# A graph layer's first stage: 16-bit one-hots of several steps, a re-timed order, one scatter per expert tile

## What is computed

```python
def gat_layer(x, W, a_src, a_dst, b, src, dst, n):
    h = x @ W
    e = leaky_relu((h @ a_src)[src] + (h @ a_dst)[dst], 0.2)
    w = exp(e - segment_max(e, dst, n)[dst])
    alpha = w / segment_sum(w, dst, n)[dst]
    return segment_sum(h[src] * alpha[:, None], dst, n) + b
def gnn(x): return gat_layer(relu(gat_layer(x, W1, ...)), W2, ...)   # self loops added
x = x + gnn(layernorm(x))
x = x + ffn(layernorm(x))      # attention of 12 heads, then top-2 of 8 experts per row, GELU
```

## Time and profile before

| | us |
|---|---|
| median of 3 runs | 1517.9 |
| profiled execution, its own time | 1517.2 |
| its span, first to last instruction | 1515.5 |
| busy: TensorE / VectorE / ScalarE / GpSimd | 1400.4 / 1146.0 / 959.7 / 502.2 |

### The profile page before, as it was taken

The page is one execution under the profiler, slowest core; times in us unless marked ns, Lnnn a source line. Parts: engine busy times, 40 slices in busy tenths (PEclk is TensorE's granted clock), DMA queues, the critical chain, the costliest instruction groups (busy, mean ns, idle before and its releaser), DMA issues.

```text
span 1515.5 us, 25550 instructions
## 1 busy us (share of the span) xinstructions
PE 1400.4 (92%) x8885; PEld 1327.4 (88%) x8885; DVE 1146.0 (76%) x1760; ACT 959.7 (63%) x1653; POOL 502.2 (33%) x366
## 2 busy tenths in 40 slices
PE   2999799999799999899999999999998997799996
PEld 1897577999799999799999999999998897699996
DVE  5788889735699863386877878778788887788885
ACT  7997787523368432275848758487587421699895
POOL 1000000000000001153635636356376410388887
PEclk9999799999999999999999999999999998799999
DMA  7001000122214540000000000000010596376642
GB/s 203 1 1 31 12 12 20 52 94 73 92 64 135 178 154 1 21 1 1 22 0 21 0 0 21 0 21 0 0 32 22 156 300 138 122 166 159 158 93 39
DMA packets 52528, 99.14 MB, mean 65 GB/s; under 512 B 11064, under 2 KB 27068, under 8 KB 52440
## 3 DMA queue, kind: packets, MB, share of 16 engines
q1 hardware_dynamic: 39985, 72.60, 15.4%
q0 software_dynamic: 11376, 22.29, 7.6%
q10 hardware_dynamic: 1079, 3.13, 0.7%
HBM read 67.15 MB, written 44.31 MB: 74 GB/s over the span
## 4 chain that ended last, share of the span: by engine, by line
PE 69%; DVE 6%; issue 3%; ACT 2%; POOL 2%; DMA 1%; ACTq 0%; POOLq 0%; SPq 0%; DVEq 0%
PE ps L376 14%; PE ps L377 14%; PE ps L378 14%; PE ps L870 5%; PE ps L915 4%; PE ps L917 3%; PE ps L894 3%; PE ps L916 3%; PE ps L896 3%; DVE mcol L1139 1%; POOL prlo L1102 1%; PE ps L616 1%; PE ps L1328 1%; DVE prlo L1102 1%; PE ps L1752 1%
## 5 line engine op out<-in xcount | busy, mean ns | idle before, releaser
L1102 POOL TENSOR_TENSOR prlo<-prob,prhi 125x500 fp32r<-125x500 f32 x180 | 260.0, 1452 | 248.4 <-ACT prob L1040 248.0
L1139 DVE TENSOR_REDUCE mcol<-ps 125x1 f32<-125x1250 f32 x120 | 174.9, 1458 | 70.1 <-PE ps L870 68.6
L1038 ACT ACTIVATE prhi<-ps 125x500 fp32r<-125x500 f32 x300 | 176.7, 589 | 70.8 <-PE ps L896 63.9
L915 PE MATMUL ps<-prhi,vhi 125*128 125x250 f32 x600 | 171.5, 286 | 10.0 <-POOL prlo L1102 6.4
L1607 POOL MEMSET q<- 128x2500 f32 x1 | 2.2, 2184 | 526.7 <-PE ps L378 526.7
L1040 ACT ACTIVATE prob<-ps 125x500 f32<-125x500 f32 x300 | 176.3, 588 | 0.7 <-DVE prlo L1102 0.6
L917 PE MATMUL ps<-prlo,vhi 125*128 125x250 f32 x600 | 167.6, 279 | 0.0
L916 PE MATMUL ps<-prhi,vlo 125*64 125x250 f32 x600 | 166.6, 278 | 0.0
L894 PE MATMUL ps<-qst,kst 128*125 128x250 f32 x600 | 155.3, 283 | 2.7 <-ACT val L569 1.1
L376 PE MATMUL ps<-hhi,pthi 125*125 125x384 f32 x400 | 153.2, 383 | 3.0 <-DVE ptlo L742 3.0
L1752 PE MATMUL ps<-ohs,ohd 128*125 128x417 bf16 x380 | 125.6, 383 | 32.3 <-DVE ohs L2194 29.5
(11 more groups left out here) (336 smaller groups left out, 3996.8 us busy)
## 6 DMA issues: line engine op xcount, KB each, us to landing
w1all<-in_L_ffn_W_dram SPq DMA_DIRECT2D x8, 1152.0 KB, 8.9
w2st<-in_L_ffn_W_dram SPq DMA_DIRECT2D x8, 1152.0 KB, 6.7
wqst<-in_L_ffn_Wqkv_dram SPq DMA_DIRECT2D x12, 384.0 KB, 4.1
hid_d<-tin SPq DMA_DIRECT2D x10, 375.0 KB
hin<-hid_d SPq DMA_DIRECT2D x10, 375.0 KB
vtin<-xn_d SPq DMA_DIRECT2D x10, 375.0 KB
out_dram<-accr POOLq DMA_DIRECT2D x10, 375.0 KB, 8.5
xres<-in_x_dram SPq DMA_DIRECT2D x10, 336.0 KB
```

The costliest lines, as they stand in the source:

```text
L915: pe.matmul(ps[:, b:b + GQ], vhi[:, e, kt, :], hi, start=kt == 0, stop=False)
L1038: act.activation(prhi[:, n % RING, :], bank(3 + n % 3, P, 2 * GQ), ACT.Exp, scale=float(HD) ** -0.5)
L1102: eng.tensor_tensor(prlo[:, n % RING, :], prob[:, n % 3, :], prhi[:, n % RING, :].bitcast(f32), ALU.subtract)\
L1139: dve.tensor_reduce(mcol[:, e, t:t + 1], ps[0:P, 0:N], AX.X, ALU.max, negate=True).then_inc(sem("max"), 1)
```

## The change

Seven things change together.

1. The source one-hots of four steps are built by one VectorE instruction on 16-bit numbers, those of the destinations of 14, 12 and 12 steps likewise; the steps lie in pairs, so that two neighbouring 2-byte elements belong to two steps and a step's operand is read with a pitch of 4 bytes. The digit value is no longer in the source one-hot: ScalarE multiplies it into each step's destination one-hot in place (`valued`). `ohs` has 3 buffers of four steps, `ohd` 4.
2. The preparation is rearranged: three fused compares with sums for the flag ahead of the digits, 16-bit copies of the column numbers, constants in another order; the edges' large loads wait for nothing and go ahead of the weights, which move from ScalarE's queue to SP's.
3. Row statistics from row tile 2 on are VectorE's (`bn_stats`, `bn_aggr`).
4. The linear starts at step 8 and takes 12 steps per row tile; turns start at step 151 and take 31 steps.
5. The first aggregated tile of layer 1 is formed in 1125 and 125 columns, and the exponential's table is loaded beforehand.
6. The second layer's weights are split from `weight2_at(k)` on, behind the last step.
7. One indirect DMA per expert tile adds all its rows; it waits for the one before.

```diff
-FIRST, PERIOD = 31, 13
-TURN0, TURN, EARLY, SLOTS = 208, 32, 12, 21
-AHEAD = 30
+FIRST, PERIOD, PARTS = 8, 12, 13
+TURN0, TURN, EARLY, SLOTS = FIRST + 143, 31, 12, 21
+AHEAD = 20
+COUNT_READY = 8
 def linear(t, r):
-    return FIRST + PERIOD * t + r
+    return FIRST + PERIOD * (PARTS * t + r) // PARTS
+def weight2_at(k):
+    return max(turn_at(7, 17) + 7 * k, STEPS + 1 + 7 * k)
...
-    ohs = put("ohs", [128, OHS, WIDE], bf16, at=WEND)
+    ohs = put("ohs", [128, SRCS, SRC_WIDE // 2, PACK, 2], bf16, at=WEND)
+    ohd = put("ohd", [128, DSTS, DST_WIDE // 2, P, 2], bf16, at=ohs_end)
+    iota2 = put("iota2", [128, PACK, 2], f16, at=put.end)
+    scol = put("scol", [128, NCOLS], f16, at=put.end)
...
 # SP
+            for a, e in ((0, src), (1, dst)):
+                sp.dma_start(eraw[:, a, 0:2, :], ...).then_inc(sem("edges_in"), 16)
             sp.wait_ge(sem("set_pool"), ERAW_CLEAR)
...
+            for m in range(2):
+                sp.dma_start(wall[:, 3 * m:3 * m + 3, :], ...)
...
 # GpSimd
-            def add_first(j):
+            def add(j):
                 pool.wait_ge(sem("y_row2"), j + 1)
+                if j >= 1:
+                    pool.wait_ge(sem(f"added{(j - 1) % 3}"), 16 * ((j - 1) // 3 + 1))
                 pool.indirect_dma_start(out=out[:, :], ..., compute_op=ALU.add,
                                         bounds_check=N - 1, oob_is_err=False)\
-                    .then_inc(sem(f"add_first{j % 3}"), 16)
-            def add_second(j):
...
 # TensorE
                 if i == 0:
-                    pe.wait_ge(sem("ohd_ready"), b + 1)
-                pe.wait_ge(sem("oh_ready"), g + 1)
-                pe.matmul(into, hots(b)[:, i, :], ohs[:, g % OHS, 0:PACK], ...)
+                    pe.wait_ge(sem("oh_ready"), b + 1)
+                pe.wait_ge(sem("valued"), g + 1)
+                pe.matmul(into, hot_dst(g), hot_src(g), ...)
...
 # ScalarE
-                last = act.activation(hots(b)[:, i, :], iota[:, 0:P], ACT.Identity, bias=drel[:, j, u:u + 1])
+                act.activation(hot_dst(g), hot_dst(g), ACT.Copy, scale=sval[:, q:q + 1]).then_inc(sem("valued"), 1)
...
+                if g == NINE + 6:
+                    sloped(act, 0, 0, 0, NINTH)
+                if g == LAST_ES + 3:
+                    sloped(act, 0, 0, NINTH, N)
+                if g == EXP_LOAD:
+                    act.activation(stat[:, 0, 0:1], viol[0:P, 3:4], ACT.Exp)
...
 # VectorE
+            def destinations(b):
+                if b >= DSTS:
+                    dve.wait_ge(sem("oh_free"), dst_start(b - DSTS + 1))
+                dve.tensor_tensor(ohd[:, b % DSTS, 0:pairs, :, :],
+                                  iota2[:, 0:P, :].rearrange("p (o c) z -> p o c z", o=1).broadcast_to([128, pairs, P, 2]),
+                                  drel[:, j, DST_AT[i]:DST_AT[i + 1]].rearrange("p (b o z) -> p b o z", o=1, z=2)
+                                  .broadcast_to([128, pairs, P, 2]), ALU.is_equal).then_inc(sem("ohd_ready"), 1)
+            def moments1(t):
+                for h in range(2):
+                    order.did(dve.bn_stats(bn[:, t % 2, 6 * h:6 * h + 6], xall[:, t, h * HALF:(h + 1) * HALF]))
+                dve.bn_aggr(lnc[:, t, 0:2], bn[:, t % 2, :]).then_inc(sem("ln"), 1)
...
             def step_near(g):
-                dve.tensor_scalar(ohs[:, g % OHS, :], iota[:, 0:WIDE], scol[:, q:q + 1], sval[:, q:q + 1], ALU.is_equal, ALU.mult)
+                if i:
+                    return
+                if b >= SRCS:
+                    dve.wait_ge(sem("oh_free"), src_end(b - SRCS))
+                dve.tensor_tensor(ohs[:, b % SRCS, 0:wide // 2, :, :],
+                                  iota2[:, :, :].rearrange("p (o c) z -> p o c z", o=1).broadcast_to([128, wide // 2, PACK, 2]),
+                                  (scodd[:, q - ODD:q - ODD + wide] if STARTS[j] % 2 else scol[:, q:q + wide])
+                                  .rearrange("p (b o z) -> p b o z", o=1, z=2)
+                                  .broadcast_to([128, wide // 2, PACK, 2]), ALU.is_equal).then_inc(sem("oh_ready"), 1)
```

More of the change, by code:

```diff
@@ L149, in build @@
     mcol = put("mcol", [P, 2, T], f32)
-    viol = put("viol", [128, 4], f32)
+    viol = put("viol", [128, 6], f32)
     FREE = top[0]
@@ L210, in build @@
     lohi = put("lohi", [128, 3, ECOLS], f32, at=put.end)
+    digit = put("digit", [128, 3, NCOLS], f32, at=put.end)
     xres = put("xres", [P, 2, D], f32, at=W2AT)
@@ L296, in build @@
     etile = put("etile", [S, TILES], i32, at=put.end)
-    index = put("index", [S, 3, TILES], i32, at=put.end)
-    later = put("later", [S, 3, TILES], f32, at=put.end)
+    index = put("index", [S, 2, TILES], i32, at=put.end)
+    later = put("later", [S, 2, TILES], f32, at=put.end)
     twice = put("twice", [P, T], f32, at=put.end)
@@ new lines, in _ @@
+            for t in range(FIRSTS):
+                moments1(t)
+            act.wait_ge(sem("start_dve"), VALUES)
+            for g in range(4):
+                valued(g)
+            weights1(0)
+            for g in range(4, 8):
+                valued(g)
+            normed(0)
+            weights1(1)
+            for g in range(8, 12):
+                valued(g)
+            weights1(2)
+            higher1(0)
+            for k in range(3, KD):
+                weights1(k)
+                valued(9 + k)
@@ L1899, in _ @@
+            for g in range(15, AHEAD):
+                valued(g)
             for g in range(SCHEDULE):
@@ new lines, in _ @@
+            s_, d_ = edge[:, 0, 0:NCOLS], edge[:, 1, :]
+            third, node, value = (digit[:, i, :] for i in range(3))
+            real = slice(LEAD, LEAD + EROWS)
+            order.did(dve.scalar_tensor_tensor(lohi[:, 0, real], d_[:, real], 0.0, lohi[:, 0, real], ALU.add, ALU.is_lt,
+                                               accum_out=viol[:, 0:1]))
+            order.did(dve.scalar_tensor_tensor(lohi[:, 1, real], d_[:, real], 0.0, lohi[:, 1, real], ALU.add, ALU.is_ge,
+                                               accum_out=viol[:, 4:5]))
@@ L2166, in rest1 @@
                     .then_inc(sem("tile_yfree"), 1)
-            def destinations(b):
-                dve.wait_ge(sem("apart"), b + 1)
-                dve.tensor_scalar(hots(b), hots(b), 0.0, None, ALU.is_equal).then_inc(sem("ohd_ready"), 1)
             def finish1(t, u):
```

376 lines of the change are left out of this document (203 added, 173 removed).

## The result

The changed kernel takes 1509.4 us (median of five runs, 1508.0 to 1511.3) where the kernel before took 1517.9: a ratio of 0.9948, interval 0.9935 to 0.9960. It is faster by 8.5 us; the forecast was 19 us (1498). The time lies inside the wide range of 1477 to 1514, and just outside the 1487 to 1508 that the prediction gave its own mechanism. The profiled execution takes 1508.7 us with a span of 1506.9. Three slow executions of two later runs (1554.9, 1756.1 and 1992.8 us) are left out of every median here.

The account below looks back on a forecast made before the run. TensorE was taken to bound the linear and the sums without steps, with a chain through three engines between. Layer 1 falls from 334.4 to 317.5 us (16.9) and scatters start 2.3 earlier: 19.2 less, 1498 us, range 1477 to 1514.

Parts of the forecast that it names:

- Start and A: Everything before the linear's first triple: first count step at 20.3 us (was 25.3), first triple at 30 (was 44.6).
- The one-hots: Count steps on VectorE: one 4-byte pair per tick, 11.7 us per 38 steps, 1.1 less than before.
- The rival of one element per 1.04 ns: Packing fails: 38 steps cost VectorE 22.4 us, total 1601 us; chance 11% for unpacked or hopping together.
- 1.73 ns per column: Hopping source in the one-hot compares: 38 steps some 7 us dearer, total about 1557; chance 11% for unpacked or hopping together.
- ScalarE: A subtraction per step traded for a scaling, 380 for 380 at 0.30 to 0.39 us: zero net.
- B: From the linear's first triple to its last, TensorE the bound: 94 us, was 95.8.
- D1: From the first triple of the sums to the last count step, TensorE becomes the bound: 136 us, was 103.0.
- TensorE's pitch: Count matmuls reading 2-byte operands at a 4-byte pitch: nothing added; a spacing above 0.18 us would show a cost.
- C: From the linear's last triple to the first triple of the sums: 27 us (22 to 32), was 37.8.
- the rival of two tied engines: VectorE and TensorE lose each other's waits: D1 141.5 us, B 100, total 1516; chance 15%.
- D2: From the last count step to layer 1's last triple: 2.65 turns without steps at 11.5, 30.5 us, was 53.2.
- the tail: Scatters behind the last matmul: one per expert tile, the last starting at 1506.4, 2.3 us earlier (3.7 earlier to 1.7 later).

## Why the prediction was right up to the last count step and wrong behind it

*Start and A: right.* 29.3 us to the first triple, 30 forecast; the edges are cast at 8.2, 7.5 forecast. That the edges' landing sets it is shown by the run with the weights ahead.

*The one-hots: right in mechanism and size.* A batch of 834 pairs took 1.017 us, as the forecast of one pair per 1.04 ns had it (1.02). The rival of one element per 1.04 ns is seen at 1.885 us where the pairs are taken away. The Trainium skill, VectorE: DVE Perf Modes, section "What auto-detection actually checks", says that a two-source operation gets two results per cycle if every tensor is 16-bit with a step of plus or minus one; both runs agree with it, since the pair gives the repeated operand such a step (1.017 us) and the lone repeated word does not (1.885). The 1.73 ns per column for a source that hops at every element, from the Trainium skill, Vector Engine (DVE) Microarchitecture Reference, section 5.2 (the SBUF access granule), does not show for a word repeated in place: a pair took 1.22 ns with the instruction's fixed part in it (1.017 us for 834).

*ScalarE: right in sum.* A scaling is 428 ns long on average, a subtraction was 390, but eleven in a row take 3.3 us, 0.30 each start to start, and ScalarE had the room (busy 69.8 of 93.0 us in B, 108.9 of 139.1 in D1).

*TensorE's pitch: a term put at nothing.* The prediction added nothing for 2-byte operands at a 4-byte pitch, because fp32 triples read 4 bytes per column at full pace, and named a spacing above 0.18 us as the sign against it. The sign came: 0.54 less 0.35 us, 0.19, where two steps follow each other, 0.18 before. At 9 ns a step that is an estimate of 2 us of D1's 228 steps.

*B and C: right.* 93.0 and 25.4 us, 94 and 27 forecast. C's granted clock stayed at 0.74 (0.73 before), where the forecast's signs had "near 1": that sign was wrong. TensorE is busy 12.8 of 25.4 us there.

*D1: between the forecast and a rival.* 139.1 us, 136 forecast and 141.5 by the rival of two tied engines. VectorE's turns start 18.8 us apart (leaky at 162.98 and six turns later at 275.62), 18 to 19 forecast. Before they started 19.2 us apart, from 196.20 to 272.92; the 17.27 of the earlier trace rows is the shortest of those four. TensorE is idle 6.0 of the 139.1 us, and the prediction's sign for tied engines, waiting mostly on ohs, came true (us in total, times, longest; changed kernel, then before):

```profile
PE ps L1798 <- DVE ohs L2275: 5.1, 5, 1.9
...
PE ps L1752 <- DVE ohs L2194: 4.9, 7, 1.5
```

It was as true of the kernel before, in a D1 of 103.0 us, so the sign does not tell the two apart. The pitch, by the estimate above, makes up some 2 of the 3 us over the forecast.

*D2: the step that failed.* The prediction priced it as "2.65 turns without steps at 11.5", 30.5 us, TensorE's own pace taken over from a stretch in which TensorE was full. For the weights' splits, now in this shorter stretch, it allowed a late load "1 to 3 us; in the range" and nothing in the sum. That allowance names the second wait (2.49 us measured). The first wait, 4.29 us, and the low clock behind it stood nowhere: the prediction compared VectorE's and ScalarE's busy time with the stretch and did not add up the chain that runs through them one link after the other. The trace after shows its length: 14.1 us from the last count step to the turn, 2.7 of them for the splits, with 18 triples, 9.85 us, of TensorE's work to cover them. Before, the turn came 30 us behind the last step, so the same links were covered. Measured: 39.0 us. Taking the splits out, reading the count in another order and reading the rows earlier brought it to 31.1; giving the chain more cover and leaving the read-back row where it was brought nothing (39.1).

That the time lies inside 1477 to 1514 is luck: none of the prediction's rivals is a chain behind the last step, and the range was not drawn for one.

*Behind layer 1.* The second linear lost 1.4 us (its pause of 0.98 among them; 79.3 us from the second row's transposes to the first turn of the next aggregation, 77.9 before), the unchanged code from there to the last result row 1.3 us, and the tail gave 2.7 where 2.3 was forecast. The tail's path was another than the one priced: the last scatter started 0.78 us behind its row and by the profile waited for that row, not for the landing of the scatter before it. With D2's 8.5 and the other stages' -0.2 this makes 8.4 + 1.4 + 1.3 - 0.4 = 10.7, the distance of the profiled execution from 1498. The 1.3 us are not explained; from that first turn to the end of the span the changed kernel and its variants spread over 1098.7 to 1105.1 us, so one execution cannot tell.

## What to carry to other kernels

When a change shortens a stage by moving work forward, list what used to be hidden behind the work that it takes away, and add up the longest chain of it, link by link over all engines, against the cover that is left (here 14.1 us against 9.85). Busy shares do not show it: VectorE was busy 16.4 and ScalarE 15.4 of the 39.0 us. A filler such as a weight split belongs behind the last link of such a chain; between two links it cost its own length plus its wait, here 2.7 us for two splits. Where two waits follow each other, shortening one can show nothing, as in two runs here (D2 38.8 and 39.1 for 39.0): take both away before judging either.

## What the runs showed of the hardware

A matmul of 417 bf16 columns took 350 ns at a pitch of 4 bytes and 341 on adjacent columns, some 9 ns more for each of 380 steps.

A wait of TensorE cost more than its length only at times, and its length alone did not tell when. After 4.29 us the granted clock was at 0.50 (302 to 304 us). After 1.88 us, in the run with the later turn, matmuls started 0.32 us apart for 3 us, and 0.18 apart after that. After 2.65 us in the same run the clock was at 0.50 again (316 to 318 us), and after 2.49 us in the changed kernel it stayed at 1.00.

The changed kernel and those of its variants whose D2 is given above pause 0.9 to 1.6 us at the second linear's first triples, a pause that the profile puts down to issue, and the kernel before does not. No run here shows what it is.
